# Perceiver layer on one core: router query matrix and keys multiplied on chip, and another order of the first two tiles

## The reference

```python
x = x + _L0_xattn_ref(_layernorm(x, axis=-1), ctx_4096, ...)   # fake_quant(x1) @ fake_quant(x2), batch by batch
x = x + _L0_attn_ref(_layernorm(x, axis=-1), ...)
x = x + _L0_ffn_ref(_layernorm(x, axis=-1), ...)

# _L0_attn_ref: q, k, v = hidden @ w.T + b, as 32 heads of 16; the heads of one row attend to each other
scores = jnp.einsum('bshd,bstd->bsht', q, k) / np.sqrt(D).astype(np.float32)
probs = jax.nn.softmax(scores, axis=-1)
context = jnp.einsum('bsht,bstd->bshd', probs, v).reshape(B, S, E)

# _L0_ffn_ref: 64 experts of rank 8, the best 16 kept
q = jnp.einsum('bsd,rd->bsr', x, Wq_w)          # Wq_w: 16 x 512
scores = jnp.einsum('bsr,er->bse', q, keys)     # keys: 64 x 16
top_vals, top_idx = jax.lax.top_k(scores, TOP_K)
...
z_gated = (z * gate[..., None]).reshape(*z.shape[:-2], BOTTLENECK)
out = jnp.einsum('bsn,on->bso', z_gated, B_w) * SCALING
```

## Time and profile before

| | |
|---|---|
| three timed runs | 162.53, 162.95, 166.27 us; median 162.95 |
| the profiled execution: device time | 163.42 us |
| its span, first to last instruction | 161.6 us |
| busy: PE, DVE, ACT, POOL | 132.2, 89.7, 60.8, 46.8 us |
| mean granted TensorE clock | 0.968 |

### The profile page before, as it was taken

How to read it: one execution, slowest core, us unless ns; L and a number is a source line. 1 busy time by engine, 2 the same in 40 slices (tenths; PEclk the granted TensorE clock), 3 DMA queues, 4 the chain that set the end, 5 groups by cost and what they waited for, 6 DMA issues and landing times.

```text
span 161.6 us, 5794 instructions
## 1 busy us (share of the span) xinstructions
PE 132.2 (82%) x2632; PEld 78.8 (49%) x2632; DVE 89.7 (56%) x183; ACT 60.8 (38%) x73; POOL 46.8 (29%) x62
## 2 busy tenths in 40 slices
PE   0069548999579589889999999999999769989993
PEld 0033437457254255365456555646544435545772
DVE  0433870076991544677973378894139439475322
ACT  0399392970174590174945303141100320211110
POOL 3235114292144159506350660010061000001000
PEclk9999999999987969987999999999999999999999
DMA  2999999999999759000001000000000000000101
GB/s 68 380 412 406 415 397 418 396 409 418 416 361 413 310 180 345 4 4 0 6 6 69 4 0 0 4 4 4 31 38 0 4 6 4 4 4 0 65 0 65
DMA packets 7099, 24.52 MB, mean 152 GB/s; under 512 B 1186, under 2 KB 1442, under 8 KB 5155
## 3 DMA queue, kind: packets, MB, share of 16 engines
q1 hardware_dynamic: 6928, 24.16, 38.4%
q10 hardware_dynamic: 146, 0.01, 0.1%
HBM read 23.11 MB, written 1.05 MB: 149 GB/s over the span
## 4 chain that ended last, share of the span: by engine, by line
PE 56%; DVE 10%; ACT 9%; issue 8%; POOL 7%; DMA 7%; SPq 1%; ACTq 0%; DVEq 0%; POOLq 0%
PE ps_b L981 17%; PE ps_a L981 15%; DMA raw<-in_ctx_dram 7%; PE ps_att L1039 5%; ACT cu L412 5%; POOL cbf L324 4%; PE ps_att L1051 3%; PE ps L1020 3%; PE ps L1105 3%; PE ps L923 2%; PE ps_t L961 2%; PE ps_t L938 2%; DVE stats L548 2%; PE ps_b L1095 1%; PE ps_a L1095 1%
## 5 line engine op out<-in xcount | busy, mean ns | idle before, releaser
L324 POOL TENSOR_SCALAR cbf<-cu 128x2048 bf16<-128x2048 uint8 x14 | 26.6, 1897 | 35.3 <-ACT cu L412 30.7
L412 ACT ACTIVATE cu<-raw,sc_in,sc_recip 128x2048 uint8<-128x2048 f32 x15 | 31.0, 2088 | 0.1
L312 POOL TENSOR_SCALAR var_eps<-mean_var 128x1 f32<-128x1 f32 x12 | 2.7, 228 | 50.3 <-DVE mean_var L550 50.1
L1039 PE MATMUL ps_att<-kT,qT 16*32 16x32 f32 x1024 | 10.9, 193 | 5.1 <-issue 5.1
L1051 PEld LDWEIGHTS ps_att<-vT,eT 32*32 32x32 f32 x1024 | 10.2, 108 | 7.3 <-issue 5.5
L1039 PEld LDWEIGHTS ps_att<-kT,qT 16*32 16x32 f32 x1024 | 9.7, 104 | 6.9 <-issue 6.7
L1051 PE MATMUL ps_att<-vT,eT 32*32 32x17 f32 x1024 | 11.4, 183 | 1.8 <-issue 1.6
L432 ACT ACTIVATE h<-x_sb,ln_shift,rstd 128x512 f32<-128x512 f32 x3 | 2.4, 813 | 24.3 <-POOL ln_shift L331 24.3
L900 PE MATMUL ps_t<-ident_bf,q 128*128 128x128 bf16 x12 | 1.4, 252 | 11.1 <-DVE q L573 11.1
L548 DVE BATCH_NORM_STATS2 stats<-x_sb 128x6 f32<-128x512 f32 x12 | 8.2, 686 | 3.5 <-POOL x_sb L341 3.2
L981 PE MATMUL ps_b<-wq,h2T 128*128 128x512 f32 x16 | 9.3, 724 | 0.7 <-ACT h2T L419 0.7
(11 more groups left out here) (127 smaller groups left out, 224.7 us busy)
## 6 DMA issues: line engine op xcount, KB each, us to landing
raw<-in_ctx_dram SPq DMA_DIRECT2D x15, 1024.0 KB, 10.4
raw<-in_ctx_dram SPq DMA_DIRECT2D x2, 512.0 KB, 11.6
wq<-in_L_attn_wq_dram SPq DMA_DIRECT2D x1, 1024.0 KB, 13.9
wk<-in_L_attn_wk_dram SPq DMA_DIRECT2D x1, 1024.0 KB, 12.8
wv<-in_L_attn_wv_dram SPq DMA_DIRECT2D x1, 1024.0 KB, 17.8
wa<-in_L_ffn_A_w_dram SPq DMA_DIRECT2D x1, 1024.0 KB, 13.0
wb<-in_L_ffn_B_w_dram SPq DMA_DIRECT2D x1, 1024.0 KB, 15.2
out_dram<-x_sb SPq DMA_DIRECT2D x3, 256.0 KB, 2.0
```

The costliest lines, as they stand in the source:

```text
L324: nc.gpsimd.tensor_scalar(cbf[:, n % BF_SLOTS, :, :], cu8[:, n % U8_SLOTS, :], -CENTER, 1.0, ALU.add, ALU.mult).then_inc(sem_ctx_bf_pool, 1)
L412: nc.scalar.activation(cu8[:, n % U8_SLOTS, :], raw[:, n % RAW_SLOTS, :], ACT.Identity, bias=sc_in[:, 3:4], scale=sc_recip[:, 2:3]).then_i ...
L1039: last = nc.tensor.matmul(ps_att[Q * j:Q * j + H, i, :], qT[rows, i, :], kT[rows, i, :], start=True, stop=True)
```

## The change

It has two parts.

One is the router. `wr` and `keys` are loaded early, before `wq`. PE transposes `wr` into the bank `ps_t1` (four transposes), ACT copies it (`copy_router_rows`), PE multiplies it with `keys` into a free part of `ps_att` (four matmuls, eight passes) and ACT copies the 512 x 64 result to `wr_keys` (`copy_router_weights`). From then on each tile's router scores are one product of h3T with `wr_keys`: eight passes of 64 columns instead of eight of 128 columns, a copy and two more passes. All of it is float32.

The other is the order of tiles 0 and 1 on PE, ACT, DVE and POOL. For the last but one step ACT also does `exp_scores(3, 1)` ahead of `exp_gates(2)`.

```diff
@@ sync
             load_x(1, 2, sem_x1_in)
+            sp.dma_start(wr[:, :, :], chunked(wrT)).then_inc(sem_router_in, 16)
+            sp.dma_start(keys[:, :], keysT).then_inc(sem_router_in, 16)
             sp.dma_start(wq[:, :, :], chunked(wqT)).then_inc(sem_wq_in, 16)
@@ gpsimd
             center_ctx(2 * BPT + 2)
-            center_ctx(2 * BPT + 3)
-            finish_norm_1(3)
             for u in range(1, TILES):
                 residual_2(u - 1)
+                if u == 1:
+                    center_ctx(2 * BPT + 3)
+                    finish_norm_1(3)
                 finish_norm_3(u - 1)
@@ scalar
-            def copy_router_q(t):
-                act.wait_ge(sem_router_q_done, t + 1)
-                if t >= 1:
-                    act.wait_ge(sem_router_done, t)
-                nc.scalar.copy(router_qT[:, :], ps1[0:RD, 0, RS:RS + P]).then_inc(sem_router_q_ready, 1)
+            def copy_router_rows():
+
+                act.wait_ge(sem_wr_transposed, 1)
+                nc.scalar.copy(wr_rows[:, :], ps_t1[0:RD, :]).then_inc(sem_wr_rows, 1)
+
+            def copy_router_weights():
+
+                act.wait_ge(sem_wr_keys_done, 1)
+                nc.scalar.copy(wr_keys[:, :, :], wr_keys_bank).then_inc(sem_wr_keys, 1)
@@
             for n in range(BPT):
                 quantise_ctx(n)
+            for i in range(3):
+                copy_bias(i)
+            copy_router_rows()
             shift_x(0)
             quantise_x(1)
-            for i in range(3):
-                copy_bias(i)
+            copy_router_weights()
             quantise_ctx(BPT)
@@
-            for n in range(BPT + 1, 2 * BPT):
+            for n in range(BPT + 1, 2 * BPT + 1):
                 quantise_ctx(n)
             exp_scores(0, 0)
-            quantise_ctx(2 * BPT)
             copy_h2T(1)
+            quantise_ctx(2 * BPT + 1)
             exp_scores(0, 1)
-            quantise_ctx(2 * BPT + 1)
             quantise_x(2)
             quantise_ctx(2 * BPT + 2)
+            quantise_ctx(2 * BPT + 3)
             copy_q1T(2)
             shift_x(2)
-            quantise_ctx(2 * BPT + 3)
@@ vector
             bias_v(0)
+            transpose_probs(0, 0)
             transpose_v(0)
-            transpose_probs(0, 0)
-            softmax_shift(0, 1)
             dve.wait_ge(sem_x_rest_in, 16)
             norm_stats(x_sb[:, 2, :], 0, 2, sem_ln1_stats, sem_ln1_mean)
+            softmax_shift(0, 1)
+            norm_1(2)
             transpose_probs(0, 1)
-            norm_1(2)
@@ tensor
+            def transpose_router_weights():
+
+                pe.wait_ge(sem_router_in, 32)
+                pe.wait_ge(sem_identity, 1)
+                for c in range(KC):
+                    last = nc.tensor.transpose(ps_t1[0:RD, c * P:(c + 1) * P], wr[:, c, :], ident[:, :])
+                last.then_inc(sem_wr_transposed, 1)
+
+            def combine_router_weights():
+
+                pe.wait_ge(sem_wr_rows, 1)
+                for c in range(KC):
+                    last = nc.tensor.matmul(wr_keys_bank[:, c * E:(c + 1) * E], wr_rows[:, c * P:(c + 1) * P],
+                                            keys[:, :], start=True, stop=True)
+                last.then_inc(sem_wr_keys_done, 1)
+
+            def router_scores(t):
                 for c in range(KC):
                     if c % (KC // 2) == 0:
                         pe.wait_ge(sem_h3T_ready, 2 * t + 2 * c // KC + 1)
-                    last = nc.tensor.matmul(ps1[0:RD, 0, RS:RS + P], wr[:, c, :], h3T[:, c, :], start=(c == 0),
+                    last = nc.tensor.matmul(ps1[:, 1, RS:RS + E], h3T[:, c, :], wr_keys[:, c, :], start=(c == 0),
                                             stop=(c == KC - 1))
@@
             product(0)
+            transpose_router_weights()
             transpose_y1(0)
+            combine_router_weights()
+            keep_clock_up(3)
             transpose_q1(1)
-            keep_clock_up(8)
             transpose_h2(0)
@@
             project_v(0, second)
+            keep_clock_up(5)
+            transpose_h2(1)
             scores(0, 1)
-            transpose_h2(1)
             project_q(1, first)
             context(0, 0)
             project_q(1, second)
-            transpose_q1(2)
             context(0, 1)
@@
                 project_k(u)
                 if u == 1:
+                    transpose_q1(u + 1)
                     product(u + 1)
```

More of the change, by code:

```diff
@@ L133, in build @@
         sem_h3T_ready = sem("h3T_ready")
-        sem_router_q_done = sem("router_q_done")
-        sem_router_q_ready = sem("router_q_ready")
+        sem_wr_transposed = sem("wr_transposed")
+        sem_wr_rows = sem("wr_rows")
+        sem_wr_keys_done = sem("wr_keys_done")
+        sem_wr_keys = sem("wr_keys")
         sem_router_done = sem("router_done")
@@ L205, in build @@
         h3T = sb("h3T", [P, KC, P])
-        router_qT = sb("router_qT", [RD, P])
+        wr_rows = sb("wr_rows", [RD, D])
+        wr_keys = sb("wr_keys", [P, KC, E])
         r_scores = sb("r_scores", [P, 2, E])
@@ L229, in build @@
         last_z = [ps_att[:, S * half:S * half + S // 2, :].rearrange("p i h -> p (i h)") for half in range(2)]
+        wr_keys_bank = ps_att[:, S:S + KC * E // H, :].rearrange("p i h -> p (i h)")
         q1_banks = [ps_t0, ps_b, ps_t0, ps_t0]
@@ L279, in _ @@
                 load_ctx(n)
-            sp.dma_start(wr[:, :, :], chunked(wrT)).then_inc(sem_router_in, 16)
-            sp.dma_start(keys[:, :], keysT).then_inc(sem_router_in, 16)
             sp.dma_start(wa[:, :, :], chunked(aT)).then_inc(sem_a_in, 16)
@@ L520, in _ @@
                     quantise_ctx(BPT * (u + 2))
-                copy_router_q(u - 1)
                 if u < TILES:
@@ L529, in _ @@
                     quantise_ctx(BPT * (u + 2) + 1)
+                if u == TILES - 1:
+                    exp_scores(u, 1)
                 exp_gates(u - 1)
-                if u < TILES:
+                if u < TILES - 1:
                     exp_scores(u, 1)
@@ L1012, in project_v @@
                 project(product_bank(2, t), h2T, wv, sem_v_done, chunks)
-            def router_q(t):
-                if t == 0:
-                    pe.wait_ge(sem_router_in, 32)
+            def transpose_router_weights():
[11 more added lines that the diff above has]
+            def router_scores(t):
                 for c in range(KC):
@@ L1019, in router_q @@
                         pe.wait_ge(sem_h3T_ready, 2 * t + 2 * c // KC + 1)
-                    last = nc.tensor.matmul(ps1[0:RD, 0, RS:RS + P], wr[:, c, :], h3T[:, c, :], start=(c == 0),
+                    last = nc.tensor.matmul(ps1[:, 1, RS:RS + E], h3T[:, c, :], wr_keys[:, c, :], start=(c == 0),
                                             stop=(c == KC - 1))
-                last.then_inc(sem_router_q_done, 1)
-            def router_scores(t):
-                pe.wait_ge(sem_router_q_ready, t + 1)
-                nc.tensor.matmul(ps1[:, 1, RS:RS + E], router_qT[:, :], keys[:, :], start=True,
-                                 stop=True).then_inc(sem_router_done, 1)
+                last.then_inc(sem_router_done, 1)
             def scores(t, part):
                 if part == 0:
+                    if t == 0:
+                        pe.wait_ge(sem_wr_keys, 1)
                     pe.wait_ge(sem_qT_ready, t + 1)
@@ L1143, in _ @@
                     transpose_y1(u + 1)
-                router_q(u - 1)
+                router_scores(u - 1)
                 project_v(u, rest)
-                router_scores(u - 1)
                 scores(u, 1)
@@ L1166, in _ @@
             transpose_h3(t)
-            router_q(t)
-            last_z_half(0, range(0, 1))
             router_scores(t)
-            last_z_half(0, range(1, KC))
+            last_z_half(0, range(KC))
             last_z_half(1, first)
```

## The result

The changed kernel takes 167.8 us (median of four runs) beside 164.6 for the kernel before in the same session: a ratio of **1.030, 95% interval 1.025 to 1.035**. It is slower, where 155.9 us and a gain of 4% were forecast. The profiled execution took 167.5 us, with a span of 165.7 where the sum of the prediction gave 154.6. (Some executions of every kernel here ran slower throughout, at a lower granted clock; the ratios leave them out, but the traces of experiments 1 to 3, of the router part in 6 and of the second variant in 8 are of such executions.) Absolute times vary by a few us between sessions, so kernels are compared by ratio.

The account below looks back on a forecast made before the run. PE was taken as the bound from about 63 us, POOL, ACT and DVE before; 161.6 - 0.7 - 5.8 + 0.85 - 0.36 - 1.0 = 154.6 us of span, forecast as 155.9 median; range 152.6 to 160.2.

Parts of the forecast that it names:

- A: From the start to scores(0,0): v(0) waits for wv and starts earlier; 0.7 us gained, bounds 1.2 lost to 1.2 gained.
- B: From scores(0,0) to h3(0): reordered tiles bring h3(0) on PE to 62.7 from 69.17; 5.8 us gained, bounds 3.2 to 6.3.
- The half stretch at 1.2 GHz: Ahead of h3(0): half of one stretch of PE at the lower clock, booked as a loss of 0.85 us.
- C: Tile 0's experts: the gate stays slow beside POOL's centring; 0 us gained, bounds 0 and 0.7.
- D: Tile 1's experts: two old router passes go, but PE waits for vT anyway; 0 us gained, bounds 0 and 0.36.
- E: Tile 2's experts: PE is the bound, so the shorter router step gains 0.36 us.
- F: Last tile: DVE starts when the eight router passes end, 150.4 instead of 151.41; 1.0 us gained, bounds 0.9 and 1.2.
- The first: Gaps inside small matmuls, scores(0,1) and scores(3,0), waits for code: 153.4 us if the second closes, chance 0.08; 158.4 if one added.
- The second rival: PE's clock, before q(0) and in waits for wv and POOL: two more stretches at 0.50, 159.3 us; chance 0.16.
- The third: ACT's reorder: copy_h2T(1) queues behind a late context 8, context(0,1) ends 2.75 us later; 158.7 us, chance 0.10.
- The fourth: POOL's swap: context 11 and h3(0) hang on context(0,1)'s end; slower from an end at 63.3, 166.3 us; chance 0.06.

Follow-up runs that it names:

- experiments 1 to 3: In order: changed kernel with wa, wb, contexts 12 to 15 held back until context(0,1), 0.968; with only wa, wb after k(1), 0.983; kernel before with the first edit, 0.990.
- the router part in 6: Kernel before with the new router alone, in the old order, with two of eight clock-keeping matmuls left: no interval, runs of 160.4 to 171.2 us.
- the second variant in 8: The version of experiment 7 with context 15 alone held back until scores(1,1): median 156.7 us, ratio 0.964 to the kernel before.
- experiment 7: Changed kernel with wa, wb and contexts 12 to 15 held back until context(0,1), without five clock-keeping matmuls ahead of h2(1), with four ahead of context(1,0): ratio 0.960.
- experiment 4: Kernel before with 16 further transfers of 1 MB, the contexts read once more from about 90 us, used by nothing: 174.8 us, ratio 1.083.
- the first of 5: Changed kernel without the five clock-keeping matmuls ahead of h2(1): ratio 1.022 to the kernel before.
- the order alone: Changed kernel with the router as it was before, keeping the new order and the clock-keeping matmuls: ratio 1.014 to the kernel before.

## Why the prediction was wrong

**What bounds the kernel:** half right. The path over ACT and POOL was the bound before, and the change did shorten it. That the supply of code lay right behind it, at nearly the same length, I didn't see, though its rows stood in the trace: 44.93 and 57.28 are two arrivals of blocks, 12.35 us for two, and my forecast wanted context(0,1) to be over at 52.2.

**A**, 0.7 forecast, 0 measured: scores(0,0) start at 38.77 (38.73 before). q(0) started at 26.69 (forecast 26.0), early enough. wv was the bound as said, but landed at 36.4, 18.4 us after its issue, instead of at 35.2: its issue slipped by 0.56 us, and it took 0.6 longer. My price for the small pieces of wr and keys was 0.5 us, and that holds: wv took 18.0 to 18.4 us in all eight kernels that load them early, and 17.5 to 17.8 in the six that don't. The later issue comes on top; over the fourteen traces it lies between 17.43 and 17.99, and what moves it isn't shown. In the other seven kernels with the early loads wv landed at 35.7 to 36.2, and still v(0) started at 36.59 or later: q(0) ran in part at 1.2 GHz there (5.7 us in experiment 7), the loss that the bounds of A name.

**B**, a gain of 5.8 forecast, a loss of 5.0 measured. This is the step that failed: it put PE's waits for its own code at nothing, on the ground that a shorter wait beside them would cover them. Up to scores(0,1) it holds: context 8 on ACT at 40.19 (forecast near 40), h2(1) transposed at 44.19 (43.45 plus the 0.7 of A). Then q(1) should end at 50.25 and ended at 59.3, and context(0,1) at 52.2 and ended at 63.4. The 11.2 us are: three waits for code, 2.84 + 2.30 + 2.02 = 7.2; passes at 1.2 GHz, 0.6 for each context half and 2.3 for the second half of q(1) (2.07 for two passes, 1.8 at full speed for four), 3.5; A, 0.7; together 11.4. Experiment 7 shows B's working up to k(1) to be right within 1.4 us: without waits for code, 53.5 and 57.1. Behind it B had v(1) at full speed, and there it lost another 1.8 us to the clock (4.52 us for six passes).

**The half stretch at 1.2 GHz**, 0.85 booked: over 15 us at half the clock, some 3.5 us of them in what B counts. It began in the first code wait. The stretches at 48 and 59 us in the kernel before had such waits ahead of them too, among others (44.93, 57.28).

**C**, 0: held. From h3(0) to the transposes of zg(0) both kernels take 12.6 us (69.17 to 81.81, 74.12 to 86.74). The gate took 1.72 us at 84.42, with a centring on POOL from 84.17; before, 1.16.

**D** and **E**, 0 and 0.36: below what can be told here. Two projections, at 87.61 and at 118.13, ran at half the clock (5.40 us for eight passes instead of 3.70), and the wait of the earlier trace rows was gone from this trace: 3.4 lost, 2.5 gained, none of it forecast. They cancel nearly, which is luck. The prediction kept that wait, because the count of passes ahead of it "hardly changes"; it changed by eight, which moved the border from 95 to 87 passes into scores(3,0).

**F**, 1.0: held, 0.9 measured, and its price for the router's eight passes too:

```profile
154.33 1.10 PE L1045 MATMUL ps<-wr_keys,h3T 128*128 128x64 f32 x8 [0.30 <-ACT h3T L442]
```

**The rivals.** The first named the right thing, and I weighed it wrongly. "The first falls where PE will wait for less anyway" treats a wait for code as idle time that a shorter wait beside it absorbs. It is a due time: the block comes when it comes, and what is moved ahead of it runs into it. I counted one more gap as the worst case (158.4), without asking at which pass the next borders lie; counted from the two that the trace showed (passes 346 and 600, 127 apart on average), they fall in context(0,0), in q(1) and two or three passes before the end of context(0,1). The chance of 0.08 was for the gap to close; for the side on which it fell I gave none of its own. The Trainium skill (Runtime: NRT & Kernel Launch, "Instruction fetch mechanics") has the block of 256 instructions, which the traces bear out: borders 126 to 128 passes apart, each pass a weight load and a matmul. It calls the crossing mostly hidden; the trace disagrees, with 2.0 to 2.8 us for each of three crossings in a row.

The second rival, the clock, came true as a consequence of the first. The third didn't: context 8 was in time. The fourth came out by its number alone. It put the point of "slower" at an end of context(0,1) at 63.3 us, with 166.3 us for the total; the end came at 63.4 and the profiled execution took 167.5, which is luck. But POOL's order isn't what held h3(0): context 11 was through at 69.21, while PE was in k(1) at 1.2 GHz up to 68.9 and waited 0.68 us for ACT's q1T, not for POOL:

```profile
69.84 1.77 PE L934 MATMUL ps<-q1T,cbf 128*128 128x33 bf16 x64 [0.68 <-ACT q1T L484]
```

I had asked what follows from a late end of context(0,1), and not what could make it late.

## What to carry over

An idle time inside a long row of small matmuls that no semaphore explains is a due time of the instruction stream, not slack: look whether a packet of the instruction queue lands just ahead of its end, count passes to find the next borders, and check that what you move doesn't reach them sooner than blocks come. Transfers that aren't needed yet cost such a stretch its code; starting them later gave 6% here without touching a computing engine. And give a wait a second price for the clock behind it, though not a fixed one: 7.2 us of waits brought 3.5 us at the lower level in the changed kernel, and 6.4 us of new waits made a span longer by 11.8 in experiment 4.

## What the runs showed of the hardware

**The pace of code.** The earlier trace rows and its like apart, where PE waited at two borders in a row, it went on 5.6 to 6.5 us after the last time with the DMA engines busy for 59% or more of the stretch (seven kernels; one case of 4.3 us), 4.8 us at 46%, and 3.6 to 4.0 us with them idle (eight kernels; in the kernel before: 134.79 - 130.79). Taken as 6.1 and 4.0 us for a block, that keeps up some 21 small passes per microsecond with the transfers and 32 without, where PE does 100 (128 in 1.29 us). The packet itself isn't what grows: it takes 0.9 to 1.6 us everywhere, and 1.1 beside the input transfers. What grows is the time until it starts: in the changed kernel the next one started 3.8 and 3.4 us after PE had gone on (50.99 to 54.76, 57.20 to 60.64), in experiment 1 1.6 us after (48.89 to 50.49, 52.89 to 54.55).

**That the waits are for code** is shown by four things together: they stand at the same passes in all kernels (346, 472, 600, 728, 981; one earlier in the router part alone), so that they move in the work with the passes put ahead of them; they have no semaphore; they follow the DMA load; and all 71 end 1.2 to 1.6 us after a packet of the instruction queue has landed. No packet started before PE was within some 20 passes of entering the block ahead of it, so that a long slow stretch stored up about one block and no more.

**A wait that stays open.** The earlier trace rows isn't explained by the pace: its border comes 13.8 us after the one at 117.00, with the DMA engines idle. It is a wait for a block all the same: the packet before it started at 114.57, and this one only at 128.16, when PE had nothing left to do (128.26). Over all fourteen kernels it appears where the border lies 95 to 97 passes into scores(3,0), with 2.0 to 2.8 us (before, experiments 3 and 4, the first of 5, the order alone), and in none of the nine in which it lies at 85 to 89 or at 98 to 99; there the packet started 5 to 10 us before PE needed the block. Why a few passes decide when it starts isn't known.

**The clock after short waits.** The wait of 2.84 us was followed by the lower level for over 15 us, with two more waits in that time. In experiment 4 waits of 1.68 and 4.40 us had the lower level behind them as well. It isn't so each time: in the order alone the clock was back at 1.00 within 4 us of the end of a wait of 3.13 us, and after the 2.53 us of the earlier trace rows it didn't fall at all (1.00 from 130 to 150 us), while the same wait in experiment 4 (2.27 us) was followed by 0.74 and 0.57 in the next two windows. What decides it isn't shown here.
